# Attention with stacked fp32 parts: keys one group ahead, both stacks loaded at a group's head, roundings on GpSimd, another order of the prologue

## The reference, cut to what matters

```python
x = x + tanh(g_xattn) * attention(layernorm(x), ctx, ctx, mask, wq, bq, wk, bk, wv, bv, wo, bo)
#   Q = layernorm(x) @ wq.T + bq ; K, V = ctx @ wk.T + bk, ctx @ wv.T + bv        (16 heads of 32)
#   attn = softmax(where(mask, -1e9, Q K^T / sqrt(32))) ; out = (attn @ V) @ wo.T + bo
x = x + tanh(g_ffn) * ffn(layernorm(x))
#   xr, xk = mu * x + (1 - mu) * previous row ; out = sigmoid(xr @ Wr.T) * (relu(xk @ Wk.T)**2 @ Wv.T)
```

## Time and profile before

| | us |
|---|---|
| median of 3 runs (1228.07 to 1229.81) | 1229.37 |
| the profiled execution | 1236.73 |
| its span, first to last instruction | 1234.9 |
| PE busy / DVE / ACT / POOL | 1150.1 / 898.0 / 722.2 / 324.1 |
| first scores of tile 0 | 37.65 |
| first `context` (b 0, group 0) | 70.26 |
| `context` of b 7, group 1 | 791.91 |
| `context` of b 7, group 2 | 815.19 |
| last `context` of stage 1 | 851.74 |
| length of a `context` on PE | 3.64 |

### The profile page before, as it was taken

One profiled execution on the slowest core, in us unless ns is written; L12 is line 12 of the kernel. 1 busy time (PEld: TensorE's weight loads), 2 busy tenths in 40 slices (PEclk: granted clock), 3 DMA queues, 4 the chain that ended last, 5 costly groups with the idle time before them and its releaser, 6 DMA issues.

```text
span 1234.9 us, 21528 instructions
## 1 busy us (share of the span) xinstructions
PE 1150.1 (93%) x7216; PEld 904.2 (73%) x7216; DVE 898.0 (73%) x1955; ACT 722.2 (58%) x1587; POOL 324.1 (26%) x518
## 2 busy tenths in 40 slices
PE   3789999999999999998999999987999999999997
PEld 3666777667767777776767776764888888888886
DVE  5667787767777777677777776779677677777763
ACT  4558678768776777676866777775432333233232
POOL 2024024023113212402402310024423433333331
PEclk9899999999999999999999999997999999999999
DMA  7654575665646567457556554662111311311300
GB/s 240 170 162 140 145 215 154 158 186 146 180 136 197 148 154 206 128 150 193 145 163 188 147 137 124 160 201 91 61 51 57 98 52 51 103 51 52 100 21 34
DMA packets 96365, 163.53 MB, mean 132 GB/s; under 512 B 13056, under 2 KB 22400, under 8 KB 96256
## 3 DMA queue, kind: packets, MB, share of 16 engines
q1 hardware_dynamic: 78112, 135.11, 37.1%
q10 hardware_dynamic: 18144, 27.04, 8.6%
HBM read 111.49 MB, written 50.62 MB: 131 GB/s over the span
## 4 chain that ended last, share of the span: by engine, by line
PE 67%; issue 9%; DVE 8%; ACT 7%; DMA 6%; ACTq 2%; POOL 0%; POOLq 0%; DVEq 0%; SPq 0%
PE bank L473 24%; PE bank L538 12%; PE bank L507 11%; PE bank L550 9%; PE bank L531 6%; ACT probs L771 3%; DMA rden_bc<-rden_dram 3%; DVE neg_s L955 3%; PE bank L516 3%; DMA rden_dram<-ctx_sb 1%; PE bank L605 1%; ACTq L761 1%; ACT pT L778 1%; DVE xh L1063 1%; DVE stats L903 1%
## 5 line engine op out<-in xcount | busy, mean ns | idle before, releaser
L771 ACT ACTIVATE probs<-neg_s,negmax 128x512 f32<-128x512 f32 x512 | 368.9, 722 | 92.3 <-DVE negmax L955 71.7
L955 DVE CUSTOM_DVE_ANT_0 neg_s<-bank,mask_big 128x512 f32<-128x512 f32 x512 | 345.4, 682 | 28.3 <-PE bank L531 20.5
L538 PE MATMUL bank<-ident,probs 128*128 128x128 f32 x2048 | 318.2, 278 | 14.1 <-ACT probs L771 11.9
L538 PEld LDWEIGHTS bank<-ident,probs 128*128 128x128 f32 x2048 | 238.6, 142 | 73.8 <-ACT probs L771 39.6
L961 DVE COPY pT<-bank 128x512 f32<-128x512 f32 x256 | 176.1, 688 | 135.2 <-PE bank L538 134.3
L531 PE MATMUL bank<-k_stack,q_stack 96*128 96x512 f32 x512 | 244.5, 478 | 24.5 <-DVE negmax L955 10.8
L778 ACT COPY pT<-bank 128x512 f32<-128x512 f32 x256 | 148.2, 579 | 131.2 <-PE bank L538 127.9
L550 PE MATMUL bank<-pT,v_sb 128*32 128x512 f32 x1024 | 117.9, 601 | 9.4 <-issue 9.0
L531 PEld LDWEIGHTS bank<-k_stack,q_stack 96*128 96x128 f32 x512 | 97.9, 191 | 31.0 <-issue 19.4
L864 ACT ACTIVATE relu<-bank 128x512 f32<-128x512 f32 x32 | 19.1, 598 | 148.8 <-PE bank L473 148.8
L771 ACT ACTIVATION_READ_ACCUMULATOR probs<-neg_s,negmax 128x1 f32 x512 | 97.4, 190 | 0.0
(11 more groups left out here) (118 smaller groups left out, 2144.0 us busy)
## 6 DMA issues: line engine op xcount, KB each, us to landing
k_stack<-qk_dram SPq DMA_DIRECT2D x96, 256.0 KB, 4.6
q_stack<-qk_dram SPq DMA_DIRECT2D x96, 256.0 KB, 4.0
cT_raw<-ctxT SPq DMA_DIRECT2D x8, 1024.0 KB, 7.9
qk_dram<-k_hi SPq DMA_DIRECT2D x32, 256.0 KB, 2.4
qk_dram<-k_lo SPq DMA_DIRECT2D x32, 256.0 KB, 3.1
qk_dram<-q_hi SPq DMA_DIRECT2D x32, 256.0 KB, 2.9
qk_dram<-q_lo SPq DMA_DIRECT2D x32, 256.0 KB, 2.5
rden_bc<-rden_dram ACTq DMA_DIRECT2D x128, 64.0 KB, 3.3
```

Of the source, the lines that this page charges most:

```text
L538: mm = nc.tensor.transpose(pt_bank[i % 2][:, a * P:(a + 1) * P], probs[:, i % P_RING, a * P:(a + 1) * P], ident[:])
L771: nc.scalar.activation(probs[:, i % P_RING, :], neg_s[:, i % SM_RING, :], ACT.Exp, bias=negmax[:, k:k + 1], scale=-1.0, accum_out=den[:, g ...
L955: nc.vector.tensor_tensor_reduce(neg_s[:, i % SM_RING, :], s_bank[i % S_BANKS][:], mask_big[:, q, :], 1.0, 3e38, ALU.add, ALU.min, negmax[ ...
```

## The change

It does six things.

1. `PE_SIDE` has another order: K is made one group further ahead (K of the group after the next in a batch's group 0, and so on), so both stacks of a group exist before the group in front of it begins or at its very beginning. A first batch has its own table, `PE_SIDE_FIRST`, in whose group 0 both K1 and K2 are made; the last batch has one K fewer. Every V quarter keeps six parts (four in group 0 of batch 0).
2. SP's program: stores of a projection and loads of bands are separate (`store`, `load_bands`); K and Q bands are loaded together at a group's head, six transfers in a row.
3. The roundings of the next batch's x and context (eight tiles of 128x512 per batch) go from ACT to POOL; `prepare_at` has no `hi` items, and the other items stand in other steps. Q4 and K4 wait for the rests block by block, and their matmuls go block by block.
4. Group 0's stacks are copied from SBUF to SBUF, head by head, 24 transfers of 32 partitions; the hi parts of Q1 and K1 on ACT wait for these copies.
5. The prologue turns x before it makes K0. The rest of wq is taken in four quarters on DVE, that of wv on POOL.
6. The rows of batch 1 for mean and variance are loaded by SP as one transfer of 1 MB into `cT_raw`.

The core of the diff:

```diff
 PE_SIDE = [
-    parts("K", 1, 0, 1, 3, 4) | parts("V", 1, 5, 6, 7, 8, 9, 10) | parts("Q", 2, 12, 13, 14, 16),
-    parts("K", 2, 0, 1, 3, 4) | parts("Q", 3, 6, 7, 8, 9) | parts("V", 2, 10, 11, 12, 13, 14, 15),
-    parts("K", 3, 0, 1, 3, 4) | parts("V", 3, 5, 6, 7, 8, 9, 10) | parts("Q", 4, 12, 13, 14, 16),
-    parts("K", 4, 0, 1, 3, 4) | parts("V", 0, 6, 7, 8, 9, 10, 11) | parts("Q", 5, 12, 13, 14, 16),
+    parts("K", 2, 0, 1, 3, 4) | parts("V", 1, 5, 6, 7, 8, 9, 10) | parts("Q", 2, 12, 13, 14, 16),
+    parts("Q", 3, 0, 1, 3, 4) | parts("K", 3, 5, 6, 7, 8) | parts("V", 2, 9, 10, 11, 12, 14, 16),
+    parts("V", 3, 0, 1, 2, 3, 4, 5) | parts("Q", 4, 6, 7, 8, 9) | parts("K", 4, 12, 13, 14, 16),
+    parts("V", 0, 0, 1, 2, 3, 4, 5) | parts("K", 5, 7, 8, 9, 10) | parts("Q", 5, 12, 13, 14, 16),
 ]
-
-
-def out_side(lag, r_step):
+PE_SIDE_FIRST = [
+    parts("K", 1, 0, 1, 2, 3) | parts("K", 2, 5, 6, 7, 8) | parts("V", 1, 9, 10, 11, 12) | parts("Q", 2, 13, 14, 15, 16),
+] + PE_SIDE[1:]
...
     first, then = nb - 2, nb - 1
     if nb == 1:
-        return {(0, 0, 0): ("rows", 0), (0, 0, 2): ("rows", 1), (0, 0, 4): ("xT", 0), (0, 0, 6): ("xT", 1),
-                (0, 0, 8): ("rows", 2), (0, 0, 10): ("rows", 3), (0, 1, 4): ("store", 0), (0, 1, 6): ("spread", 0),
-                (0, 1, 14): ("hi", 0), (0, 1, 15): ("hi", 1), (0, 2, 1): ("xT", 2), (0, 2, 2): ("xT", 3),
-                (0, 2, 7): ("hi", 2), (0, 2, 8): ("hi", 3)}
-    return {(first, 3, 0): ("rows", 0), (first, 3, 2): ("rows", 1), (first, 3, 4): ("xT", 0), (first, 3, 6): ("xT", 1),
-            (first, 3, 10): ("rows", 2), (first, 3, 12): ("rows", 3), (then, 0, 12): ("store", 0),
-            (then, 0, 14): ("spread", 0), (then, 1, 10): ("hi", 0), (then, 1, 12): ("hi", 1), (then, 1, 14): ("xT", 2),
-            (then, 2, 0): ("xT", 3), (then, 2, 4): ("hi", 2), (then, 2, 6): ("hi", 3)}
+        return {(0, 0, 0): ("xT", 0), (0, 0, 2): ("xT", 1), (0, 0, 14): ("store", 0), (0, 1, 1): ("spread", 0),
+                (0, 1, 14): ("xT", 2), (0, 2, 0): ("xT", 3)}
+    return {(first, 3, 0): ("rows", 0), (first, 3, 2): ("rows", 1), (first, 3, 10): ("rows", 2),
+            (first, 3, 12): ("rows", 3), (first, 3, 14): ("xT", 0), (then, 0, 2): ("xT", 1), (then, 0, 12): ("store", 0),
+            (then, 0, 14): ("spread", 0), (then, 1, 10): ("xT", 2), (then, 1, 12): ("xT", 3)}
...
-PROLOGUE = C_ITEMS + [("K", 0)] + T_ITEMS + [("Q", 0), ("V", 0), ("Q", 1)]
+PROLOGUE = C_ITEMS + T_ITEMS + [("K", 0), ("Q", 0), ("V", 0), ("Q", 1)]
+NEXT_BATCH = [("Q", 4), ("K", 4), ("V", 0), ("Q", 5), ("K", 5)]
...
+            def copy_rows(which, j, bands, source):
+
+                for band in bands:
+                    sp.dma_start(stack[0][which][HD * band:HD * (band + 1), j, :].bitcast(F32),
+                                 source[which][HD * j:HD * (j + 1), :].bitcast(F32)).then_inc(copied[which][j], 16)
+
+            sp.wait_ge(side_done, done(side_no(None, ("C", CH - 1))))
+            sp.dma_start(cT_raw[:], x[bass.ds(S, S), :].rearrange("(p t) c -> p t c", t=TT)).then_inc(rows1_ld, 16)
+            sp.wait_ge(side_done, done(side_no(None, ("K", 0))))
+            for j in range(GH):
+                copy_rows(1, j, (0, 2), qk_hi)
+                copy_rows(1, j, (1,), qk_lo)
+                if j == 0:
+                    sp.wait_ge(side_done, done(side_no(None, ("Q", 0))))
+                copy_rows(0, j, (0, 1), qk_hi)
+                copy_rows(0, j, (2,), qk_lo)
...
+            def store(b, kind, n):
+
+                which = "QK".index(kind)
                 g = n if b is None else b * GROUPS + n
+                sp.wait_ge(side_hi, hi_no(b, (kind, n)) + 1)
+                sp.dma_start(qk_dram[g, which, 0], qk_hi[which][:].bitcast(F32)).then_inc(part_st[which][0], 16)
+                sp.wait_ge(side_done, done(side_no(b, (kind, n))))
+                sp.dma_start(qk_dram[g, which, 1], qk_lo[which][:].bitcast(F32)).then_inc(part_st[which][1], 16)
+
+            def load_bands(g, kind):
+
+                which = "QK".index(kind)
                 sp.wait_ge(s_mm, (g - 1) * TILES + HEAD)
+                for part in range(2):
+                    sp.wait_ge(part_st[which][part], g * 16)
+                    for band in range(BANDS):
+                        if ((0, 0, 1), (0, 1, 0))[which][band] == part:
+                            sp.dma_start(stack[g % 2][which][HD * band:HD * (band + 1), :, :].bitcast(F32),
+                                         qk_dram[g, which, part].rearrange("(j d) t -> d j t", j=GH)).then_inc(
+                                             stacked[which], 16)
...
                 for c in range(GROUPS):
-                    if not (is_last(b) and c == GROUPS - 1):
-                        if is_last(b) and c == GROUPS - 2:
-
-                            sp.wait_ge(side_mm, mm_no(b, ("Q", c + 1)) + 1)
+                    g = b * GROUPS + c
+                    if c == 0:
+                        store(*((b - 1, "Q", 5) if b else (None, "Q", 1)))
+                        if b:
+                            load_bands(g + 1, "K")
+                        load_bands(g + 1, "Q")
+                        if b == 0:
+                            store(0, "K", 1)
+                            load_bands(1, "K")
+                        store(b, "K", 2)
+                    if c == 1:
+                        store(b, "Q", 2)
+                        load_bands(g + 1, "K")
+                        load_bands(g + 1, "Q")
+                        store(b, "Q", 3)
+                        store(b, "K", 3)
+                    if c == 2:
+                        if not more:
                             load_w2(0)
-                        stack_group(b, c + 1)
-                    if b + c:
+                        load_bands(g + 1, "K")
+                        load_bands(g + 1, "Q")
+                        if more:
+                            store(b, "Q", 4)
+                    if c == 3 and more:
+                        store(b, "K", 4)
+                        load_bands(g + 1, "Q")
+                        load_bands(g + 1, "K")
+                        store(b, "K", 5)
...
-                if part == 0 and (kind, n) == ("Q", 4):
-                    pe.wait_ge(x_lo, (b + 1) * CH)
-                if part == 0 and (kind, n) == ("K", 4):
-                    pe.wait_ge(ct_lo, (b + 1) * CH)
+                if (kind, n) == ("Q", 4):
+                    pe.wait_ge(x_lo, b * CH + part + 1)
+                if (kind, n) == ("K", 4):
+                    pe.wait_ge(ct_lo, b * CH + part + 1)
...
+                if kind in "QK" and g == 1:
+
+                    for heads in copied["QK".index(kind)]:
+                        act.wait_ge(heads, BANDS * 16)
+                if kind in "QK" and g > 1:
...
+            def split_wq():
+                dve.wait_ge(w_hi_done, 2)
+                for a in range(CH):
+                    nc.vector.scalar_tensor_tensor(out=w1_lo[0][:, a, :], in0=pT[:, 0, a], scalar=-SCALE,
+                                                   in1=w1_hi[0][:, a, :], op0=ALU.mult,
+                                                   op1=ALU.subtract).then_inc(wq_lo_done, 1)
...
+            def x_rounded(b, a):
+                pool.wait_ge(x_hat, (b - 1) * CH + a + 1)
+                pool.wait_ge(side_mm, mm_no(b - 1, ("Q", GROUPS - 1)) + 1)
+                nc.gpsimd.tensor_copy(act_hi[0][:, a, :], x_rows[:, 2 + a % 2, :]).then_inc(x_hi, 1)
...
+            def c_rounded(b, a):
+                pool.wait_ge(c_ld, b * 16 + 16)
+                pool.wait_ge(side_mm, mm_no(b - 1, ("V", 3)) + 1)
+                nc.gpsimd.tensor_copy(act_hi[1][:, a, :], cT_raw[:, a, :]).then_inc(ct_hi, 1)
...
+            pool.wait_ge(w_hi_done, 3)
+            nc.gpsimd.tensor_tensor(w1_lo[2][:], pT[:, 2], w1_hi[2][:], ALU.subtract).then_inc(wv_lo_done, 1)
...
+                        x_rounded(b, a)
+                    for a in pair:
                         x_rest(b, a)
-                for a in range(CH):
-                    c_rest(b, a)
+                c_rounded(b, 0)
+                for a in range(1, CH):
+                    c_rounded(b, a)
+                    c_rest(b, a - 1)
+                c_rest(b, CH - 1)
```

More of the change, by code:

```diff
@@ L244, in build @@
         stacked = [sem(f"{n}_stacked") for n in "qk"]
+        copied = [[sem(f"{n}_copied_head{j}") for j in range(GH)] for n in "qk"]
+        rows1_ld = sem("rows1_ld")
         pv_mm = sem("pv_mm")
@@ L263, in build, with number @@
         out_st = [sem("out_st0"), sem("out_st1")]
+        def number(b, item, kinds):
+            at = 0 if b is None else b + 1
+            before = sum(len([i for i in order if i[0] in kinds]) for order in ORDERS[:at])
+            return before + [i for i in ORDERS[at] if i[0] in kinds].index(item)
         def side_no(b, item):
[L267 to L270 removed]
+            return number(b, item, "CTKQVR")
         def side_bank_of(b, item):
@@ L292, in listed @@
```

(15 more changed lines are left out.)

219 lines of the change are left out of this document (85 added, 134 removed).

## The result

The changed kernel is slower: median 1238.82 us (six runs, 1235.93 to 1240.22) against 1229.59 for the kernel before in the same session (six runs, 1228.07 to 1234.08), a ratio of 1.0061 with a 95% interval of 1.0038 to 1.0085. The forecast was 1206.3, so it was wrong, in sign too.

The account below looks back on a forecast made before the run. PE sets the pace, idle 32.87 us in 29 groups. Steady part -19.3, up to the first context -3.5, end of stage 1 -0.3: -23.1 from the median 1229.37 gives 1206.3 us; range 1197 to 1219.

Parts of the forecast that it names:

- Stacks at the head: Stage 1: six bands issued by about a group's first tile end late-band waits (-3.6 us) and most tile 14 waits (-7.5).
- (a): Stage 1, tile 14 of a group: PE waits for a minimum of DVE, 8.5 us in 8 waits; 1.0 left.
- R3: Rival: six bands hold ACT's queue at the head, 1.1 us in each of 31 groups; 1237 us, chance 0.07.
- steady part: First `context` to that of b 7, group 1: -22.0 of 32.9 us idle, 2.7 against for new collisions; -19.3.
- (b): Stage 1, next group's first scores: PE waits for late-issued key bands, 3.6 us in 3 waits; all to go.
- Roundings on GpSimd: Stage 1: casts at 1.29 us on POOL stay hidden; -4.0 at tile 15, -3.4 more with transfers' new places.
- R2: Rival: POOL casts take 1.8 us, so blocks come late for K4, 7 times; +8 to +12, 1216; chance 0.06.
- End of a group: Stage 1, before `context`: a V part in step 16 of group 1 and shorter earlier waits save 3.5 of 8.0 us.
- (d): Stage 1, before `context`: PE waits for a tile's last copy, 8.0 us in 16 waits, mostly 0.48.
- Prologue: Up to the first `context`: -3.5 us, bounds 0 and -7; first scores at 35.6, first `context` near 66.8.
- The collision: Prologue: POOL's subtraction of wv's rest holds DVE's fourth quarter of wq until POOL is done, 4.5 us.
- End of stage 1: b 7, group 2 loses its K, 2.8 us of PE, but tiles without side parts wait for ACT: -0.3 us.

Follow-up runs that it names:

- e_poolb: The kernel before with only the eight roundings per batch moved from ACT to POOL; 1224.62 us, ratio 0.9918 against the kernel before.

## Why the prediction was wrong

**The step that failed** is the one under "Stacks at the head": "The middle of the group is left to the spread [...]: of (a) I leave 1.0, -7.5", and with it the reason set against R3, that the bands "need some 6 us" and the sums are stored after. The bands do leave 2.05 us before the first tile (524.51 to 526.56), but they are not alone: one load of x rows and the stores of `k_hi` and `k_lo` go in front of them, a second load of x rows comes behind them, and the engines are full until 534.0, 9.5 us after the first band's issue. And the sums are stored at 530.89, 4.3 us after the first tile and not 5.5, in the middle of this traffic. I counted the bands and left out their company, though I had named the company for (a) in the kernel before. PE's waits of that kind moved from tile 14, behind DVE's divide, to tile 8, behind ACT's exponential: 21.6 us and the lower clock after three of them, where I had left 1.0. So the steady part, forecast at -19.3, came out at +1.7 (723.34 against 721.65). The experiments give it 28 to 30 us (1.0061 against 0.9834 and 0.9813), and with it mended the changed kernel has 0.9813 x 1229.59 = 1206.6, within 1 us of the forecast. That closeness is partly luck, see the next three points.

**The base.** The sum took the waits of one execution for the kernel's. That execution was 7.4 us above the median, and a second one, 5.4 us shorter, has 3.4 us less of (b) and 1.9 less of (a). I took these waits off, and then took the 7.4 off as well: by these two traces some 5 us were counted twice.

**Roundings on GpSimd.** The cover held and K4 never waited; a cast took 0.61 us, the lower bound and not my 1.29, so R2 had no ground. The Trainium skill's 769 ns ("GPSIMD Engine Reference", section 3.1, there as the best case of a tight loop) is too high for this cast, which took 609. Its verdict against elementwise work on GpSimd is one against VectorE, where no run here has this cast; what counted here is that the operation takes as long as on ACT, and that the engine was idle. The worth of this part was undervalued: 10 us in e_poolb, where my -4.0 and a part of -3.4 stood.

**End of a group.** (d) fell from 8.0 to 1.4 us, more than the 3.5 taken. The two bare steps at 10 and 11 were missed, though the table in the diff shows them: 7.2 us.

**Prologue.** The collision came as forecast: the quarters took 6.83 us instead of 2.28, 4.6 too long (4.5 forecast), and the first scores came at 36.06 (35.6 forecast). Mis-sized was the issue of the 18 copies, for which I took the 0.42 us of a 256 KB load: a copy of 32 partitions takes 0.61 us of SP's queue and the 18 took 11.4 us (34.66 to 46.02) instead of 7.6, so that Q1's rounding began at 47.66 instead of 43.2, and the lower clock followed. Forecast for the first `context` 66.8, measured 71.40.

**End of stage 1.** b 7, group 2 takes 21.65 us where I had 23.04; forecast -0.3, measured -1.6.

**The rivals.** R3's time, 1237, was nearly the measured one, and its engine, ACT, was right. Its cause was another: not the issue of the transfers at steps 0 to 4 but a receipt at step 6, not 31 groups but 14. So that its time came out is partly luck. (Its sum takes 26.6 us as gained; the terms of the forecast add up to 25.8.) It had 0.07. What spoke for R3, that nothing in the trace has six bands at once, should have weighed more than an estimate of 6 us which no row of such a burst carried. The last line of the prediction did name the right sign, ACT standing at steps 6 to 8, though it stood so in 14 groups and not in most.

## What to carry to other kernels

An instruction that waits for a transfer's receipt costs what stands behind it in its queue: place it as far behind the store as the receipt takes when the DMA engines are full (here 3 to 6.6 us for 8 KB, 1.35 when they were quiet), or keep large transfers from being issued before it. When transfers are moved, add up all bytes that are issued ahead of the small transfer, stores and other queues' loads too, and not those of the moved ones alone. And take waits as a kernel's own only when a second execution shows them: what makes one execution longer than the median can't be both taken off as a wait and subtracted with the median.
